# Second attention of a fused transformer kernel: the vector engine's place for the next tile's norm

## The reference

```
x = x + L1_ffn(layernorm(x))                      # the feed-forward block before
# the third layer's attention, called a2 and "second attention" in the kernel
q = layernorm(x) @ Wq.T + bq                      # 16 heads of 8 features
k, v = ctx @ Wk.T + bk, ctx @ Wv.T + bv
s = q k' / sqrt(8) + causal mask
x = x + softmax(s) v @ Wo.T + bo
h = layernorm(x)                                  # input of the next feed-forward block
```

## Time and profile before

| | us |
|---|---|
| median of 3 runs | 847.32 (846.9 to 849.75) |
| the profiled execution, its own time | 847.17 |
| its span in the profile | 845.1 |
| PE busy | 807.0 (95%) |
| DVE busy | 634.4 (75%) |
| ACT busy | 563.0 (67%) |
| POOL busy | 286.8 (34%) |

### The profile page before, as it was taken

One profiled execution on the slowest core, in us unless ns is written; L12 is line 12 of the kernel. 1 busy time (PEld: TensorE's weight loads), 2 busy tenths in 40 slices (PEclk: granted clock), 3 DMA queues, 4 the chain that ended last, 5 costly groups with the idle time before them and its releaser, 6 DMA issues.

```text
span 845.1 us, 20299 instructions
## 1 busy us (share of the span) xinstructions
PE 807.0 (95%) x7358; PEld 565.4 (67%) x7358; DVE 634.4 (75%) x1586; ACT 563.0 (67%) x1598; POOL 286.8 (34%) x587
## 2 busy tenths in 40 slices
PE   8999999999999999899999999999999989899986
PEld 8887888899998987554444444444466665676652
DVE  5678777777777665766966967756999967899876
ACT  3666667777767776686455666465577779888654
POOL 4246444455444335200000000002156630435445
PEclk9999999999999999999999999999999999999999
DMA  8700000000000000000000000000000000000000
GB/s 337 170 2 1 1 1 2 1 2 1 1 2 2 2 1 2 1 0 1 1 0 1 1 1 0 1 0 1 1 28 4 3 3 1 3 3 3 2 28 26
DMA packets 7886, 13.54 MB, mean 16 GB/s; under 512 B 4342, under 2 KB 5100, under 8 KB 7532
## 3 DMA queue, kind: packets, MB, share of 16 engines
q1 hardware_dynamic: 7788, 12.24, 4.6%
HBM read 11.19 MB, written 1.05 MB: 14 GB/s over the span
## 4 chain that ended last, share of the span: by engine, by line
PE 68%; DVE 14%; ACT 8%; issue 5%; POOL 4%; DMA 1%; DVEq 0%; POOLq 0%; SPq 0%; ACTq 0%
PE psum L1561 10%; PE psum L772 7%; PE psum L812 6%; PE psum L840 6%; PE psum L755 5%; PE psum L764 3%; ACT arena L910 2%; PE psum L1547 2%; PE psum L1570 2%; PE psum L2016 2%; PE psum L790 2%; PE psum L2401 2%; PE psum L829 2%; PE psum L2523 2%; PE psum L1986 2%
## 5 line engine op out<-in xcount | busy, mean ns | idle before, releaser
L517 POOL TENSOR_TENSOR ve<-mv,epsv 128x1 f32<-128x1 f32 x176 | 35.7, 203 | 422.0 <-DVE mv L512 422.0
L1561 PE MATMUL psum<-arena,w1f 128*128 128x512 f32 x240 | 109.5, 592 | 0.0
L520 POOL TENSOR_TENSOR rstd<-ve,epsv 128x1 f32<-128x1 f32 x176 | 101.3, 575 | 13.8
L910 ACT ACTIVATE arena<-psum,negmax 128x128 f32<-128x128 f32 x256 | 90.3, 405 | 22.2 <-DVE negmax L1010 22.2
L1561 PEld LDWEIGHTS psum<-arena,w1f 128*128 128x128 f32 x240 | 45.5, 190 | 48.6 <-issue 44.3
L1100 POOL TENSOR_TENSOR arena<-arena,rsum 128x512 f32<-128x512 f32 x64 | 65.7, 1046 | 24.6 <-DVE rsum L1016 24.6
L1010 DVE TENSOR_REDUCE negmax<-psum 128x8 f32<-128x1024 f32 x32 | 39.2, 1225 | 32.9 <-PE psum L812 32.9
L910 ACT ACTIVATION_READ_ACCUMULATOR arena<-psum,negmax 128x1 f32 x256 | 63.0, 246 | 0.0
L526 DVE TENSOR_SCALAR yln<-x_tok,mv,rstd 128x128 f32<-128x128 f32 x128 | 56.7, 454 | 7.9 <-POOL rstd L520 7.5
L755 PE MATMUL psum<-arena,sclA 128*128 128x128 f32 x512 | 62.5, 275 | 0.1
L772 PE MATMUL psum<-arena 128*128 128x512 f32 x128 | 61.5, 599 | 0.9 <-DVE arena L1005 0.6
(11 more groups left out here) (375 smaller groups left out, 1968.3 us busy)
## 6 DMA issues: line engine op xcount, KB each, us to landing
w<-in_w0qk SPq DMA_DIRECT2D x2, 512.0 KB, 4.9
w<-in_w0vo SPq DMA_DIRECT2D x1, 1024.0 KB, 7.6
cT<-in_cT SPq DMA_DIRECT2D x1, 1024.0 KB, 14.7
out<-x_tok SPq DMA_DIRECT2D x4, 256.0 KB, 2.2
rows<-in_rows SPq DMA_DIRECT2D x1, 836.0 KB, 12.3
x_tok<-in_x_tok SPq DMA_DIRECT2D x1, 768.0 KB, 9.7
ctx_tok<-in_ctx_tok SPq DMA_DIRECT2D x1, 768.0 KB, 10.9
wa<-in_wa SPq DMA_DIRECT2D x1, 768.0 KB, 16.8
```

Of the source, the lines that this page charges most:

```text
L520: pool.tensor_tensor(rstd[:, u, self.i:self.i + 1], ve[:, u, self.i:self.i + 1], epsv[:, 1:2], ALU.pow) \
L910: m = nc.scalar.activation(e0[:, b, g, :], ps(k, P, j * P), ACT.Exp, bias=negmax0[:, b, g:g + 1], accum_out=sum0[:, b, g:g + 1])
L1561: nc.tensor.matmul(ps(k), w1("e2", j * 384 + arg * D, j * 384 + (arg + 1) * D), f1_Hm[:, n, 2 * j + i, :], start=False, stop=False)
```

## The change

In DVE's list `apply` (lag 0) moves from the end of the step to the place directly behind `s`, the subtraction of the maxima. It is now ahead of `rsum`, `stats` and `av`. No instruction is added or removed, and no wait is written anew. `apply` for the tiles 0 to 5 stands in the list written by hand and stays where it is, so that the tiles 6 to 15 are touched, in the steps 6 to 15.

```diff
-        ATT_DVE = [("own", 0), ("max", 4), ("tail", 8), ("add", 7), ("s", 4), ("rsum", 6), ("stats", 7), ("av", 6), ("apply", 0)]
+        ATT_DVE = [("own", 0), ("max", 4), ("tail", 8), ("add", 7), ("s", 4), ("apply", 0), ("rsum", 6), ("stats", 7), ("av", 6)]
```

## The result

| | before | after |
|---|---|---|
| median of 19 runs each, us | 846.88 (844.97 to 849.75) | 844.81 (842.87 to 847.62) |
| ratio | | 0.9979, 95% interval [0.9971, 0.9988] |
| the profiled execution | 847.17, span 845.1 | 847.62, span 845.5 |
| DVE busy | 634.4 | 629.2 |

The change saves 0.21% (0.12 to 0.29), 1.8 us of 846.9 (1.0 to 2.5). The forecast was 1.37 us, and 845.95 us for the median, 1.14 over the measured 844.81. Of that difference 0.44 us is the starting point: the forecast stood on the median of 3 runs (847.32), that of 19 runs is 846.88.

The account below looks back on a forecast made before the run. DVE's load was taken to set eight steps of about 4.82 us, with the ring next at 4.69. Savings of 0.48 and 0.89 us make 1.37, taking the median from 847.32 to 845.95 us; range 844.3 to 847.9, given 84%.

Parts of the forecast that it names:

- The forecast of 1.37 us: Whole kernel: 0.48 us saved in the step from 625.87 and 0.89 in the seven after it; given 76%.
- The ring is late next, at 4.69 us: DVE `add`, subtraction, PE's scores to `out`, back to `add`: sets the step at 4.69 us once DVE has time to spare.
- the 0.48 us under 4.94: Step from 625.87, without `lnt` in the ring: `add` moves from 629.39 to 628.91, 0.48 us saved.
- `apply` falls into POOL's pause at 0.34 us: Behind the subtraction, `apply` ends 0.34 us before `km` starts, so it takes 0.34 us instead of 0.96.
- Its own wait: Moved `apply` needs POOL's root, which is ready 0.59 us ahead in the ring's shorter step: no wait.
- bank 6: `av` on DVE frees it 0.25 us later against the subtraction; 0.29 us remain before PE's `v`, so nothing waits.
- DVE's slack of 0.46 us: Changed steps: DVE reaches `add` before PE's `out` is due, with some 0.45 us to spare in a step.
- Of 6.25 us freed most turns into idle time: Ten `apply` free 6.25 us on DVE; 1.37 us shortens the kernel, the other 4.9 become DVE idle time.
- DVE's load costs about 0.12 us a step: Eight slow steps of the kernel before: DVE full at 4.75 of 4.82 us, against 4.69 in the next two.
- The full 6.25 us: Rival: DVE is the bound and PE is not, so all 6.25 us come out, 841.1 us; 5%.
- `tail` at 0.38 us: Rival: `tail` meets POOL's two L620 and gives back 0.8 us, 846.75; 13% together with nothing gained.
- The slower case: Rival: `km` holds `apply` in the new place, PE's `v` waits for bank 6, some +4 us, 851.3; 6%.

Follow-up runs that it names:

- the swap of `lnt`: Changed kernel with PE's `lnt` ahead of its scores instead of behind them: 0.9965 of the kernel before, median 843.41 us, steps of 4.60 us.
- the swap of `lnt` in the kernel before: Kernel before with PE's `lnt` put ahead of its scores: 0.9975 of the kernel before, steps of 4.72 us but for one of 4.93.
- the load kernels: Changed kernel with one, two, three or five extra moments instructions on DVE in steps 6 to 15: steps of 4.69, 4.69, 4.78 and 5.16 us.
- the second experiment: Against the changed kernel, `apply` moved to between `stats` and `av`, just ahead of `km`: 0.9980 of the kernel before.

## Why the prediction was right, and where its reason was not

- The forecast of 1.37 us lies in what was measured (1.0 to 2.5). The nine steps together are 1.20 us shorter (43.09 to 41.89); most of what lacks to 1.37 is the one step of 4.81. The profiled execution loses 0.3 us again at 682 us, in the last steps: PE stands idle for 0.86 us within the 64 small matmuls of one `av` (L2035), where it was 0.58 in the kernel before. So the traces place 1.2 us, or 0.9 with this loss, of the measured 1.8; the rest is not placed.
- *The ring is late next, at 4.69 us.* Right: six of the nine steps are at 4.69 or 4.70, the two without `lnt` at 4.44 and 4.46 (the second is the 0.48 us under 4.94 that the prediction had), and the swap of `lnt` moved it to 4.60.
- *`apply` falls into POOL's pause at 0.34 us.* Right in all ten, from 619.61 to 661.50. L526 takes 6.50 us in 18 instructions between 620 and 667 us, where it was 12.37; now they are nine `apply` (0.34) and nine `tail` (0.38 to 0.40), before they were ten and eight. The prediction had 6.1, with `tail` at 0.34.
- *Its own wait, bank 6, DVE's slack of 0.46 us.* Right; the slack measured 0.50, and PE never stopped for bank 6 in the steady steps. The idle time ends with PE's `out`, as it had said, though the profile puts it down to POOL's L620 in five of eight steps.
- *Of 6.25 us freed most turns into idle time.* Right: DVE's busy time in all is 5.2 us less, the time some 1.8.
- *"DVE's load costs about 0.12 us a step".* Wrong in its cause. The 0.12 us was right as a difference of two rows, but what set the old step was a ring of two steps through `km` and the hold, where DVE's work between the subtraction and `apply` is free (0.39 us more of it changed nothing). A held instruction counts as busy, and so DVE looked full. The forecast stood because moving `apply` takes the hold, the link between `km` and DVE, out of that ring altogether, and the next ring was read from its own rows. That the wrong cause did no harm is partly luck: the same picture gave the wrong answer for the swap of `lnt` in the kernel before.
- *The rivals.* The full 6.25 us didn't come (at most 2.5), and the load kernels show why: DVE had 0.50 us to spare in a step, so it wasn't the bound. `tail` at 0.38 us cost nothing in the changed kernel, but it did where `km` was split. The slower case needs `km` to be first in the new place, and it never was.

## What to carry to other kernels

When an engine looks full, look at whether one of its instructions ends at a fixed distance behind another engine's: then part of its busy time is a wait, and the bound may be the ring through that other engine, perhaps over more than one step (steps that alternate around a mean are a sign of it). Look for a place outside the ring where the other engine pauses (here directly behind the subtraction), and price the gain by the next ring, read from a step where the first doesn't bind. A move on one engine is safe only when the bank that it writes and the copies that stand behind it have been followed: the same transpose gained 1.2 us ahead of the scores and lost 5 behind `out`.

## What the runs showed that was not expected

PE stops inside a row of equal small matmuls now and then, in some kernels and not in others: in the step of 4.81 us of the changed kernel the eight matmuls of L2001 took 0.58 instead of 0.45 (the kernel before has the same, hidden in its longer step), in the step of 5.09 of the second experiment 0.85; with one extra instruction on DVE no step shows it. In the second experiment the weight loads show a gap that no semaphore explains:

```profile
643.84 0.31 PEld L2001 LDWEIGHTS psum<-wa,cT 128*64 128x64 f32 x7
644.43 0.13 PEld L2001 LDWEIGHTS psum<-wa,cT 128*64 128x64 f32 x1 [0.28 <-issue]
```

It costs 0.1 to 0.4 us where PE is in the ring. Its cause wasn't tried. One lead: five of the fourteen traces show the stop, all at the same L2001 (646.41 us in the kernel before, 643.94 in the changed one), and in all five a transfer of an instruction queue starts 2.05 to 2.07 us ahead of it. But other L2001 with such a transfer as far ahead don't stop, so the transfer alone is not shown to be the cause.

The runs of one kernel spread by more than the change is worth, and the granted clock goes with it: of the 19 runs of the changed kernel the nine with a mean clock of 0.998 or more have a median of 843.7 us (842.9 to 844.7), the ten below 845.5 (844.8 to 847.6). The 47 runs of the kernel before that were measured beside the experiments divide in the same way: 845.5 us for the 18 at 0.998 or more, 847.4 for the 29 below. At like clock the change is worth 1.8 to 1.9 us, so the clock's scatter is not what makes the gain. Why the clock dips in one run and not in the next stays open.
